# State-space stage with channels on partitions: a one-core Trainium2 kernel of four layers

## What is computed

```
proj = hidden @ in_proj_w.T                    # gate (4096), hbc (4096 + 1024 + 1024), dt (64)
xBC  = silu(causal convolution of hbc, 4 taps, + conv_bias)    # x, B, C
dt_p = softplus(dt + dt_bias); dA = exp(-dt_p * exp(A_log))
state = state * dA_t + dt_p * x_t B_t          # for each head and token t
y_t   = state . C_t + x_t * D
y     = y * rsqrt(mean over the 512 channels of a group of y*y + eps) * norm_weight
out   = (y * silu(gate)) @ out_proj_w.T
```

## Time and profile before

| | us |
|---|---|
| three runs | 1831.64, 1835.91, 1842.42 |
| median | 1835.91 |
| the profiled execution, its own time | 1837.23 |
| its span, first to last instruction | 1835.4 |
| first transposes of the first group (stage begins) | 81.3 |
| first transposes of the last group | 958.6 |
| last output tile of the stage added | 1099 |

### The profile page before, as it was taken

The page is one execution under the profiler, slowest core; times in us unless marked ns, Lnnn a source line. Parts: engine busy times, 40 slices in busy tenths (PEclk is TensorE's granted clock), DMA queues, the critical chain, the costliest instruction groups (busy, mean ns, idle before and its releaser), DMA issues.

```text
span 1835.4 us, 25172 instructions
## 1 busy us (share of the span) xinstructions
PE 1620.2 (88%) x8696; PEld 1272.0 (69%) x8696; DVE 1297.8 (71%) x2037; ACT 755.8 (41%) x1389; POOL 1006.7 (55%) x861
## 2 busy tenths in 40 slices
PE   3699989999999999999999877997489999988692
PEld 2478768777877787778777656886356676767581
DVE  5687888787888778787778856555636776768525
ACT  2443433434434434434343213333136766664231
POOL 3376775776767767757766835003433443328554
PEclk9899999999999999999999978999589999998696
DMA  4001020020010010200201001212000000032344
GB/s 134 1 35 47 1 79 3 0 80 0 34 46 0 34 46 0 80 0 0 80 0 43 38 1 64 69 69 92 0 0 13 1 13 1 1 147 83 100 142 160
DMA packets 23303, 79.73 MB, mean 43 GB/s; under 512 B 6464, under 2 KB 6592, under 8 KB 17984
## 3 DMA queue, kind: packets, MB, share of 16 engines
q1 hardware_dynamic: 19552, 66.73, 10.1%
q0 software_dynamic: 3680, 12.06, 2.0%
HBM read 68.56 MB, written 10.22 MB: 43 GB/s over the span
## 4 chain that ended last, share of the span: by engine, by line
PE 66%; DVE 13%; POOL 7%; issue 6%; ACT 4%; DMA 3%; SPq 1%; POOLq 0%; DVEq 0%; ACTq 0%
PE banks L344 35%; PE banks L1597 6%; PE banks L1529 3%; PE banks L1716 3%; PE banks L1607 2%; PE banks L1538 2%; PE banks L1496 2%; DMA x<-in_w_conv 2%; PE banks L1675 2%; POOL wol L349 2%; PE banks L1706 2%; DVE acc L558 2%; POOL am L640 1%; DVE nmax L1322 1%; DVE tap L1100 1%
## 5 line engine op out<-in xcount | busy, mean ns | idle before, releaser
L640 POOL TENSOR_TENSOR am<-ah,upto 128x1024 fp32r<-128x1024 f32 x64 | 129.3, 2021 | 217.9 <-PE banks L1496 203.6
L1100 DVE SCALAR_TENSOR_TENSOR tap<-banks,parg,tap 128x511 f32<-128x511 f32 (+2 forms) x288 | 214.9, 746 | 30.3 <-ACT tap L856 23.5
L1176 DVE TENSOR_TENSOR em<-em,gmask 128x1024 f32<-128x1024 f32 x64 | 129.3, 2020 | 91.4 <-ACT em L889 90.9
L791 POOL TENSOR_SCALAR kz<-kst,head 128x512 fp32r<-128x512 f32 x64 | 99.1, 1568 | 160.0 <-DVE kst L1306 160.0
L344 PE MATMUL banks<-xTh,wch 128*128 128x512 f32 x384 | 166.4, 433 | 3.7 <-POOL wcl L349 2.4
L640 POOL TENSOR_TENSOR am<-al,upto 128x1024 fp32r<-128x1024 f32 x64 | 160.7, 2511 | 0.0
L344 PE MATMUL banks<-xTh,wcl 128*128 128x512 f32 x384 | 151.7, 395 | 0.0
L344 PE MATMUL banks<-xTl,wch 128*128 128x512 f32 x384 | 151.4, 394 | 0.0
L1032 ACT ACTIVATE prob<-banks,nmax 128x128 f32<-128x128 f32 (+3 forms) x256 | 121.8, 530 | 54.5 <-DVE nmax L1322 54.3
L1529 PEld LDWEIGHTS banks<-dtx,em 128*128 128x128 f32 x1024 | 123.2, 192 | 23.0 <-issue 21.3
L1322 DVE TENSOR_REDUCE nmax<-banks 128x2 f32<-128x256 f32 (+3 forms) x128 | 104.7, 818 | 40.4 <-PE banks L1707 40.3
(11 more groups left out here) (289 smaller groups left out, 4471.3 us busy)
## 6 DMA issues: line engine op xcount, KB each, us to landing
x<-in_w_conv SPq DMA_DIRECT2D x7, 1536.0 KB, 6.6
x<-in_w_gate SPq DMA_DIRECT2D x8, 1024.0 KB, 4.8
x<-in_w_out SPq DMA_DIRECT2D x8, 1024.0 KB, 6.8
eraw<-in_expert_w SPq DMA_DIRECT2D x8, 1024.0 KB, 7.2
gur<-in_ff_gu SPq DMA_DIRECT2D x7, 1024.0 KB, 4.8
x<-in_hidden SPq DMA_DIRECT2D x16, 256.0 KB, 4.3
mates<-yd SPq DMA_DIRECT2D x8, 512.0 KB, 4.3
dnr<-in_ff_dn SPq DMA_DIRECT2D x7, 512.0 KB, 3.5
```

Source lines behind the costliest of these rows:

```text
L640: m = pool.tensor_tensor(am[:, part, :, :], a[:, i, :].bitcast(F32).unsqueeze(2).to_broadcast([P, HG, P]), upto[:, :].unsqueeze(1).to_broa ...
L791: m = pool.tensor_scalar(kz[:, quad % 2, p2, j, :], kst[:, p2, :].bitcast(F32), head[:, j:j + 1], None, ALU.mult)
L1100: nc.vector.scalar_tensor_tensor(tap[:, q % 2, sh:L], bk(CONV_BANKS[q % 2])[:, 0:L - sh], parg[:, KC * q + k:KC * q + k + 1], tap[:, q % 2 ...
L1176: nc.vector.tensor_tensor(em[:, s % 2, :, :], em[:, s % 2, :, :], gmask[:, :].unsqueeze(1).to_broadcast([P, HG, P]), ALU.mult).then_inc(m_ ...
```

## The change

The second half of the stage is turned. Tile i's output `y` now has the 128 channels of two heads on partitions, in four blocks, and tokens along the free axis:

- The mixer product takes each head's 64 columns of `dtx` as stationary operand and moves the head's mixer matrix past it; even heads write partitions 0 to 63 of bank 7, odd heads 64 to 127. The state read becomes four products with a block of the state stationary.
- The decays on entry vary along the free axis now. They are computed as a head-by-token table in the prologue, stored to device memory (`grownT`), and SP loads those of one tile, repeated over 64 partitions, into `grown` ahead of each use, by two DMAs (`grown_load`), six tiles a group.
- The skip term is a product with a value for each partition, straight from the convolution's output, in four pieces on VectorE; POOL's `xd` is gone.
- The sum of squares: ScalarE squares, POOL adds four blocks to one in two additions, TensorE sums over partitions by a product with a column of ones, ScalarE scales it and adds epsilon, POOL takes the root. The root is applied last, where VectorE adds the output product to `acc`; so `y` times gate goes straight to the split and the output product, and the four transposes of `yn` are gone.
- The gate is made for a channel block and a sequence at a time, weights stationary, and kept for all of a group. One is made in each step, the first three of a group in the last three steps of the group before (of the first group in the prologue). So gate weights are cast and split in step 5; their staging buffer is shared with the output weights, which are loaded after that.
- In steps without convolution tiles VectorE's product with the decays on entry stands before the mask product `em`; in all steps the low half of the output stands before it.

```diff
-            sp.dma_start(out_stage, w_out[0]).then_inc(wo_in, 16)
+            def grown_load(g, i):
+                at_least(sp, yo_used, entered(g, i) + i % CH - 1)
+                for u in range(2):
+                    sp.dma_start(grown[HP * u:HP * u + HP, :, :],
+                                 halves[u][bass.ds(g, 1), :, i * P:(i + 1) * P].rearrange("g k t -> (g k) t").partition_broadcast(HP)
+                                 ).then_inc(grown_in, 16)
+            sp.wait_ge(dt_act, 7)
+            sp.dma_start(grownT.rearrange("h (b t) -> h b t", b=NB), xtok[0:H, :, :]).then_inc(grown_out, 16)
+            sp.wait_ge(wg_lo, KT)
+            sp.dma_start(out_stage, w_out[0]).then_inc(wo_in, 16)
...
             with sp.Fori(0, G - 1) as g:
-                sp.wait_ge(wg_lo, KT * g + KT)
+                grown_load(g, 1)
+                grown_load(g, 2)
                 sp.wait_ge(wo_lo, KT * g + KT)
                 sp.dma_start(conv_stage(1), w_conv[bass.ds(g + 1, 1)]).then_inc(wc_in, 16)
+                grown_load(g, 3)
                 sp.wait_ge(wc_lo, 2 * g + KT + 2)
                 sp.wait_ge(wc_lo2, 2 * g + KT + 2)
                 sp.dma_start(gate_stage, w_gate[bass.ds(g + 1, 1)]).then_inc(wg_in, 16)
+                grown_load(g, 5)
+                sp.wait_ge(wg_lo, KT * g + 2 * KT)
                 sp.dma_start(out_stage, w_out[bass.ds(g + 1, 1)]).then_inc(wo_in, 16)
+                grown_load(g, 6)
+                grown_load(g, 7)
...
# POOL, step
+                if not (first and s < 2):
+                    n = NT * g + s - 1
+                    pool.wait_ge(sq_ready, n)
+                    pool.tensor_tensor(ysq[:, 0:2, :], ysq[:, 0:2, :], ysq[:, 2:4, :], ALU.add).then_inc(sum_ready, 1)
+                    pool.wait_ge(sum_ready, 2 * n - 1)
+                    pool.tensor_tensor(ysq[:, 0, :], ysq[:, 0, :], ysq[:, 1, :], ALU.add).then_inc(sum_ready, 1)
+                if s == 5 and not last:
+                    gate_low(g + 1)
...
-                if s < NT:
-                    if not (first and s == 0):
-                        pool.wait_ge(y_ready, NT * g + s)
-                    pool.tensor_tensor(pair(xd[:, :]), src, heads(5 * NT), ALU.mult).then_inc(xd_ready, 1)
...
# ScalarE, step
+                if not (first and s < 2):
+                    act.wait_ge(yn_ready, NT * g + i + 1)
+                    at_least(act, o_ready, NT * g + i)
+                    nc.scalar.copy(ynTh[:, :, :], y[:, :, :]).then_inc(ynT_hi, 1)
+                if s == 5 and not last:
+                    gate_high(g + 1)
...
-                    nc.scalar.activation(sg[:, s % 2, :], y[:, :], ACT.Square, scale=float(GI) ** -0.5,
-                                         accum_out=ss[:, (s - 1) % 2:(s - 1) % 2 + 1]).then_inc(ss_ready, 1)
+                    nc.scalar.activation(ysq[:, :, :], y[:, :, :], ACT.Square).then_inc(sq_ready, 1)
...
# VectorE, step
+                def entered_part():
+                    at_least(dve, ynT_lo, NT * g + i)
+                    if c > 0:
+                        dve.wait_ge(yo_ready, m + c)
+                        dve.wait_ge(grown_in, 32 * (m + c))
+                        nc.vector.tensor_tensor(y[:, :, :], kt(bk(6)), grown, ALU.mult).then_inc(yo_used, 1)
+                def skipped(base):
+                    for k in range(KT):
+                        n = nc.vector.scalar_tensor_tensor(y[:, k, :], xbc[:, k, i % NT * P:(i % NT + 1) * P], skipg[:, k:k + 1],
+                                                           base[:, k, :], ALU.mult, ALU.add)
+                    n.then_inc(y_ready, 1)
...
+                if not (first and s < 2):
+                    dve.wait_ge(ynT_hi, NT * g + s - 1)
+                    low(nc.vector, ynTl[:, :, :], y[:, :, :], ynTh[:, :, :]).then_inc(ynT_lo, 1)
+                if s < NT:
+                    if s > 0 and not tiles:
+                        entered_part()
                     dve.wait_ge(e_ready, NT * g + s + 1)
...
-                    nc.vector.tensor_tensor(acc[:, i % NT, :], acc[:, i % NT, :], bk(1), ALU.add).then_inc(out_added, 1)
+                    dve.wait_ge(rg_ready, NT * g + i + 1)
+                    nc.vector.scalar_tensor_tensor(acc[:, i % NT, :], bk(1), rg[:, i % 2:i % 2 + 1], acc[:, i % NT, :],
+                                                   ALU.mult, ALU.add).then_inc(out_added, 1)
...
# TensorE, step
-                    for j in range(KT):
-                        m = pe.transpose(bk(4)[:, j * P:(j + 1) * P], yn[:, j * P:(j + 1) * P], ident[:, :])
-                    m.then_inc(yn_tr, 1)
+                    mat(bk(4)[:, 0:1], ysq[:, 0, :], ones[:, 0:1], start=True, stop=True).then_inc(ss_ps, 1)
...
-                        mat(bk(6), xbc[:, JC, tok], state[:, :], start=True, stop=True).then_inc(yo_ready, 1)
+                        for j in range(KT):
+                            m = mat(bk(6)[:, j * P:(j + 1) * P], state[:, j * P:(j + 1) * P], xbc[:, JC, tok], start=True, stop=True)
+                        m.then_inc(yo_ready, 1)
...
                     for h in range(HG):
-                        m = mat(bk(7)[:, h * HP:(h + 1) * HP], em[:, i % 2, h, :], dtx[:, h * HP:(h + 1) * HP],
-                                start=True, stop=True)
+                        m = mat(bk(7)[h % 2 * HP:h % 2 * HP + HP, h // 2 * P:(h // 2 + 1) * P], dtx[:, h * HP:(h + 1) * HP],
+                                em[:, i % 2, h, :], start=True, stop=True)
...
+            def gated(b, j, bank):
+                ch, tok = slice(j * P, (j + 1) * P), slice(b * L, (b + 1) * L)
+                products(bk(bank), [(wgh[:, k, ch], wgl[:, k, ch], xTh[:, k, tok], xTl[:, k, tok])
+                                    for k in range(KT)]).then_inc(gate_ready, 1)
```

253 lines of the change are left out of this document (152 added, 101 removed).

## The result

The changed kernel takes 1825.26 us (median of 6 runs, 1824.15 to 1826.55) against 1836.7 for the one before (median of 6): a ratio of 0.9947, 95% interval 0.9928 to 0.9965. (The two medians by themselves give 0.9938.) It is faster, by half a per cent. The forecast was 1752 us with a range of 1720 to 1802, so the kernel is 73 us slower than forecast and outside the range. The profiled execution took 1824.79 us.

The account below looks back on a forecast made before the run. TensorE, busy 88% of the span, was taken to bound the kernel. From 1837.2 us, 63 came off for six middle groups, 2 for first group with prologue, 20 for the last: 1752 us, range 1720 to 1802.

Parts of the forecast that it names:

- TensorE's terms: Per step on TensorE: 0.44 us from transposes plus 0.59 from the mixer product, less 0.28 for sum of squares: 0.75 gained.
- The upper bound of the mixer product: Mixer product with its instructions one after another, 1.74 us plus 0.26 for the switch: a loss of 0.27 us a step.
- Rival 1: Mixer product: the pairs of 64-column strips do not overlap, a step gains -0.11 us, total 1800 us; chance 0.14.
- the transfers: New DMAs of the decays, six times a group, used 10 to 16 us after issue: cost 0 and no gain.
- Rival 3: The decays' transfers land late for L1186 in six steps of each group, up to 1944 us; chance 0.04.
- Do the others keep up?: Per step: VectorE some +0.6 us with a cover of 1.9, POOL -0.4, ScalarE busy half the time or less.
- the state product need not wait: Eighth step: L1186 stands ahead of the mask product, so the 0.86 us idle goes and the step takes 10.7.
- rival 2: VectorE or POOL becomes the bound; tile steps cost VectorE 2.5 us more and gain nothing: 1790 us; chance 0.15.
- The steps: A group's eight steps: six with tiles 92.7 us, fourth 12.3, eighth 10.7; 115.7 against 126.2, -10.5 a group.
- First group and prologue: Prologue +6.5 us for three gate products and low halves, first group's steps -8.5: together -2 us.
- the last group: Last group: fourth step -6 us, last stretch from 52.5 to 39, -13, the others -1: -20 us.
- rival 4: New hand-overs between engines (squares, root, gate, output) cost each step what it saves: 1837 us; chance 0.05.

Follow-up runs that it names:

- e11: The changed kernel with e5's and e9's edits, and all four low halves of the next convolution weights on VectorE, none on GpSimd: 1753.15 us, ratio 0.9553.
- e13: e11 with the mixer product's heads in the order 0 2 4 6 1 3 5 7, so that no pair overlaps: 1772.1 us, ratio 0.9665.
- e7: The changed kernel with the mixer product's heads in the order 0 2 4 6 1 3 5 7, so that no pair overlaps: 1819.33 us, ratio 0.9906.
- e8: The changed kernel with VectorE's two low halves of the next convolution weights cut to 8 columns, mostly old data: 1801.42 us, ratio 0.9806.
- e9: The changed kernel's prologue reordered: gate casts ahead of ScalarE's first taps, gate low halves ahead of GpSimd's first decays: 1818.17 us, ratio 0.9901.
- e5: The changed kernel with masked product of B and C, skip term and gated output all kept in PSUM: 1765.91 us, ratio 0.9623.
- e2: The changed kernel with the masked product of B and C written back to PSUM bank 5, where the mask product reads it: 1788.18 us, ratio 0.9753.
- e12: The changed kernel with only all four low halves of the next convolution weights moved to VectorE: 1841.85 us, ratio 1.0052.

## Why the prediction was wrong

**Right: TensorE's terms.** The tile steps that TensorE alone bounds went from 15.91 to 14.93 and 15.12 us and from 16.81 to 15.96, 0.8 to 1.0 a step where 0.75 was forecast. The mixer product takes 1.02 (forecast 1.14), the state read 1.00 (0.88), the sum of squares 0.12 in e11's and e13's chains and in most of this kernel's (0.28). The three errors, 0.12 to 0.16 us, partly cancel. The upper bound of the mixer product was too high: without the overlap it takes 1.51, not 1.74 plus 0.26. How much of that is the switch and how much the 0.11 a product isn't shown.

Rival 1 fell with e7 and e13: pairs do overlap, and taking that away lengthens the product by half (1.02 to 1.51).

**Right: the transfers.** The 128 KB loads land 4.7 us after issue (the page), and L1271, which uses them, has no wait released by a DMA. Rival 3 didn't come.

**Wrong: the step "Do the others keep up?".** It gave VectorE 0.6 us more a step and a cover of 1.9. The middle groups show 1.6 more. The low half was priced at the median of L1202, 0.95 us; in its new place it takes 1.38. The skip pieces were priced by a row that reads PSUM (0.28) and take 0.56 with both inputs in SBUF. And the mask product, not touched by the change, went from 2.02 to 2.22. Busy time over the stage, by 64 steps, gives the skip term +0.75 us a step (forecast +0.17), the low half +0.70 (+0.27), VectorE's two low halves of the convolution weights +0.26 and the mask product +0.20 (both forecast at nothing), less some savings elsewhere. The row that told of this was in the prediction: L1202 between 0.69 and 4.38. Its median was the wrong figure twice over. A sum needs the mean, which was 1.15; and either belongs to the arrangement of the kernel before, in which GpSimd came to wait for L1202 in 31 of 48 cases.

**Wrong: "the state product need not wait".** The prediction put the wait of the eighth step at nothing, because L1186 now stands ahead of the mask product, and gave the third none. In the middle groups TensorE waits ahead of the state product in the third, fourth and eighth step, 1.4 us each time and 25.7 us in all (203 to 900 us), for L1271, L1186's successor. What stands before L1271 is the stretched low half (2.21 us in the eighth step shown), and in the third step the stretched mask product too (2.81 us).

That is rival 2's mechanism, which the prediction gave a chance of 0.15 and 1790 us. Its size was wrong too: it let VectorE's extra time eat no more than the gain of the tile steps, so that the fifth would be back at its 15.9 us. It takes 20.4 in the mean. By the Trainium skill's rule ("SBUF — State Buffer", SBUF: two separate sides), this was the case to expect, and the trace now agrees more closely than the earlier trace rows seemed to: VectorE's and GpSimd's pairs of low halves take 1.86 and 3.69 us one after the other, 4.55 and 4.40 beside each other, 5.2 us from first start to last end, so hardly less than the 5.55 of their sum. In e8 an operation of 0.15 us ended only when GpSimd's did.

**Wrong: "The steps", fourth and fifth.** The forecast for third to fifth was 43.5 us (16.1 + 12.3 + 15.1). The group shown takes 51.1. The third and fourth were reckoned from GpSimd's load of 28.4 us; in fact GpSimd was busy 25.97 of their 29.88, and VectorE 12.37 of the fourth's 12.70. The forecast counted GpSimd's skip product as 1.15 us saved. The wait for L1202 ahead of it, and the root behind it, were also what kept GpSimd's low halves behind VectorE's. Without them the two pairs collide, TensorE waits 3.3 us for the bank that VectorE frees behind them, and the granted clock over the step is 0.84. The fifth step alone makes 5.3 of the 8.3 us that a middle group is over its forecast. e8 gives the price of VectorE's two low halves: 3.3 us a group.

**Wrong: first group and prologue.** +11.3 us of prologue in place of +6.5, and -1.2 in the first group in place of -8.5. The idle time that was to hide some of the gate products didn't: TensorE waited 4.7 us for their low halves, which GpSimd could not make before ScalarE's casts. The prediction moved GpSimd's low halves ahead, but didn't ask when ScalarE would cast. e9 took 7.8 us off the stage's start, gave 2.4 back in the first group, and the time went from a ratio of 0.9947 to 0.9901. The first group lost its forecast gain in the same steps as the others (its third takes 19.65 us and its fifth 20.23).

**Half right: the last group.** -10.1 us (140.98 to 130.91) in place of -20. Here TensorE waits 11.4 us, five times, for GpSimd's sums ahead of the sum of squares (L1632), and 5.5 and 3.8 us for VectorE's L1271 and low half. The first is one of rival 4's new hand-overs, which the prediction took to be over in time.

**The sum of the misses:** middle groups 49.8 (13.2 gained of 63), last group 9.9, first group 7.3, prologue 4.8, the rest of the program 0.7: 72.5 of the 72.8 that lie between 1752 and 1824.8. e11 comes out at 1753.15 us, once VectorE reads PSUM in three places, the low halves are placed apart and the prologue is reordered. Its middle groups are what the forecast had (693.2 us against 757.2 - 63 = 694.2), but that the whole agrees is partly luck: its prologue and first group are 3.3 us shorter than forecast and its last group 6.1 longer.

**Left open:** what share of e7's 6 us is the phase of VectorE against GpSimd and what the clock; how far the last group could be brought towards its forecast, which no run tried by itself (125.5 us in e5, 121 forecast); and whether the skip product and the root kept the two pairs of low halves apart as the timelines suggest, since no run put them back.

## What to carry to other kernels

Before an operand moves from PSUM to SBUF, or a partner's work from one engine to another, list for each VectorE operation with two SBUF inputs what GpSimd does in the same microseconds, and price it at the row's maximum where they meet, not at its median. A wait that disappears may have been what kept two such operations apart. If an engine is late by such stretches, writing an intermediate result back into its PSUM bank is a cure of a few lines (three in e2, one of them TensorE's wait for the bank), and it can pay in a kernel whose bottleneck seems to be elsewhere (25 us in the kernel before).

## What the runs showed that was not expected

VectorE's operations with one input in PSUM held their duration whatever GpSimd did: a mean of 686 or 687 ns for L1245's 512 columns in every run after the change, 746 for the output sum (739 to 752 over 64 times in the changed kernel). With both in SBUF, 768 columns took 0.94 to 1.00 us where GpSimd had only an operation of one column beside them, and 2.59 to 2.68 beside its low halves or its products for the decays. GpSimd is stretched too: in the changed kernel its products for the decays take 1.89 at least, 2.34 in the median for the second one and 2.88 at most.

More of a saving on VectorE showed in the time than expected: e2 took 64 us from one group of VectorE's operations and 37 from the time, though TensorE was busy for 93% of the middle groups. e12 and e7 surprise the other way: two low halves a group moved from the stretched GpSimd to VectorE cost 17 us, and more work for TensorE gained 6.
